# Two buffers for delta, du and B and C by the chunk's parity, in a Mamba, expert and attention kernel

## The chip, the core and the metric

The kernel runs on one core of a Trainium2 chip. The metric is the device time of one execution in microseconds; lower is better. The engines are TensorE (PE, with its weight loads PEld), VectorE (DVE), ScalarE (ACT), GpSimd (POOL) and SyncE (SP, which issues the DMAs).

## The reference

Two sequences of 2048 tokens with 256 features pass through four layers, each with a residual and a layer norm. The change is in the first:

```python
xz = xn @ W_in
x_br, z = jnp.split(xz, 2, axis=-1)
# xc: causal convolution of x_br with 4 taps
xb = jax.nn.silu(jnp.transpose(xc, (0, 2, 1)))
Bm = xb @ W_b
Cm = xb @ W_c
delta = jax.nn.softplus(xb @ W_delta + b_delta)
A_bar = jnp.exp(delta[..., None] * A)
Bx = delta[..., None] * Bm[:, :, None, :] * xb[..., None]
def step(h, inp):
    a_t, bx_t, c_t = inp
    h = a_t * h + bx_t
    y_t = jnp.sum(h * c_t[:, None, :], axis=-1)
    return (h, y_t)
...
out = y * jax.nn.silu(z) @ W_out
```

Behind it come a mixture of four experts (a router, then per expert two products with a Gelu between, all four computed and weighted), the projections q, k and v of a 16-head attention, the attention itself, and a last feed-forward layer.

## The kernel before

The first stage (`mamba_moe_qkv`, the first 1800 us) goes through 8 chunks of 512 tokens. The inner width of 512 stands on the partitions as four blocks of 128. An iteration i works on up to four chunks at once: the scan of chunk i, the front part of chunk f = i+1 (norm, `project_x`, `conv`, `project_bc`, `project_delta`, softplus), output projection, router and experts of chunk m = i-1, and the projections q, k, v of chunk q = i-2. Iterations run from -1 to 9; 3 to 5 are one loop, the others are written out. Each engine's program is one fixed order, written by hand, and waits on semaphores.

An iteration has 16 slots n, one per state of the scan:

- VectorE in slot n, for each of four blocks: `b_times` (L1231), du times B's row, which lies in a PSUM bank, and `scan` (L1238) over 512 steps with the decays. Between block 1 and 2 ("the middle") and behind block 3 and `keep_state` (L1244, "the end") stands other work: `down` (L1316, adds an expert's output to the sum), `gated` (L1250, y times the gate, middle of slot 0), `norm1_stats` (L1256 and more, middle of slot 2), `conv` (L1191), `keys` (L1333, the added keys, middle of slot 7), `weigh` (router weights, end of slot 6), `split_bias` (L1344, end of slot 9), `split_bc` (L1199 to L1206, end of slot 14: B and C as three bf16 parts into `bc3`), `deltas` (L1216, two halves, then du in two halves, L1222; end of slot 15).
- TensorE in slot n: parts of the projections and experts. `up` (L722) fills three PSUM banks in turn, which ScalarE empties by Gelus (L1005); `down` (L746) follows. `broadcast(c, n)` (L598) spreads row n of B over the partitions. It waits until VectorE has used row n-2, since two banks alternate. Slot n ends with the broadcast of row n+2; rows 0 and 1 of the next chunk come at the end of slot 15.
- ScalarE in slot n: first the decays (L913) of slot n+1, which need VectorE's scan of slot n-1 for their buffer, then copies and Gelus. In slots 12 to 14 `copy_delta` (L965, L966) writes the projected delta into `pre` and its absolute value into `soft`, and `soft_exp`, `soft_log` make the softplus' second term.
- GpSimd in slot n: `times_c` (L1437), h times C's row, and `add_y` (L1448), both four instructions, once VectorE has ended slot n. VectorE's scan of slot n waits for `add_y` of slot n-2; `gated` waits for that of slot 15.

`delta`, `du` and `bc3` have one buffer. So `deltas` has to wait for the chunk's last decays and last `b_times`, and `split_bc` for its last broadcast. The decays of the next chunk wait for both halves of `deltas`. The buffer `soft` also serves chunk q: `cr` (the cross products), `kb_f` (a bias per head); `kb_parts` has its own.

`START` gives, for iterations 8 and 9, how many products of the first attention heads are put between; the change leaves it alone.

## Time and profile before

| | us |
|---|---|
| median of 3 runs | 3821.85 (3819.26 to 3822.27) |
| the profiled execution | 3819.2, its span 3817.4 |
| first stage, of the span | about 1830 |
| PE busy over the span | 3385.6 (89%) |
| DVE busy | 2945.8 (77%) |
| ACT busy | 2222.2 (58%) |
| POOL busy | 1508.8 (40%), nearly all of it in the first stage |
| granted TensorE clock, mean | 0.95 |

An engine's busy time over the whole span is a mean over two stages with different limits; the change touches the first alone. Four views of it are used: the instructions of one line in a stretch (when an iteration begins), the busy time in a stretch, the waits of an engine (who ended them, how long), and the timeline, where each row is a run of instructions of one line, with its start, its length and, in brackets, the idle time ahead of it and what ended that.

### The profile page before, as it was taken

To read this page: it belongs to the slowest core of one execution; us is meant where nothing else is said; L and a number is where in the kernel's file an instruction comes from. 1 tells how busy PE (TensorE), PEld (TensorE's weight loads), DVE (VectorE), ACT (ScalarE), POOL (GpSimd) and SP (SyncE) were. 2 spreads that over 40 slices of the span, in tenths; PEclk is the share of its full clock that TensorE was granted. 3 is DMA by queue.
4 is the path that set the end of the run, shared out by engine and by line. 5 is a ranking of instruction groups with operands and counts; after the bars stand their busy time and mean duration, and the time that the engine had idled before them with its cause. 6 is when DMAs were issued, how large, how long until landed. Compare 5 with 4: busy or idle time off the path is not lost. (4 is left out here: it accounts for less than half of the span.)

```text
span 3817.4 us, 50051 instructions
## 1 busy us (share of the span) xinstructions
PE 3385.6 (89%) x14561; PEld 1587.7 (42%) x14561; DVE 2945.8 (77%) x3571; ACT 2222.2 (58%) x3640; POOL 1508.8 (40%) x1294
## 2 busy tenths in 40 slices
PE   4339899898888989899979999999999999999998
PEld 1115555454554546455533232323232323233666
DVE  5898797978879787985438888888788888887343
ACT  5345565656556565553127777777677777776221
POOL 3988787887878788885010000000000000000110
PEclk8669999999999999999989999999999999999999
DMA  2111122122222212223111000000000000001010
GB/s 104 32 38 61 56 71 91 61 87 72 72 65 75 85 61 83 70 80 127 56 46 50 18 18 18 18 18 18 19 18 18 18 18 18 18 18 35 22 33 28
DMA packets 111209, 183.03 MB, mean 48 GB/s; under 512 B 14623, under 2 KB 84663, under 8 KB 102393
## 3 DMA queue, kind: packets, MB, share of 16 engines
q1 hardware_dynamic: 110969, 180.13, 14.9%
q8 instruction: 114, 1.87, 0.2%
q14 instruction: 126, 1.03, 0.1%
HBM read 153.99 MB, written 26.09 MB: 47 GB/s over the span
## 5 line engine op out<-in xcount | busy, mean ns | idle before, releaser
L1894 DVE TENSOR_REDUCE tile_max<-ps 128x1 f32<-128x1024 f32 x1028 | 1210.9, 1220 | 253.3 <-PE ps L1685 250.5
L1835 ACT ACTIVATE probs<-ps 128x512 f32<-128x512 f32 x2056 | 1115.9, 598 | 374.4 <-PE ps L1699 348.7
L1437 POOL TENSOR_TENSOR vals<-vals,c_sb 128x512 f32<-128x512 f32 x512 | 673.0, 1346 | 275.9 <-DVE state L1244 275.8
L1238 DVE TENSOR_TENSOR_SCAN vals<-stacks,state,ps 128x512 f32<-128x512 f32 x512 | 655.0, 1279 | 99.2 <-POOL heads_v L1448 28.1
L1699 PE MATMUL ps<-stacks 101*128 101x512 bf16 x2056 | 708.1, 382 | 13.6 <-ACTq L1842 12.4
L1448 POOL TENSOR_TENSOR heads_v<-heads_v,vals 128x512 f32<-128x512 f32 x512 | 638.9, 1280 | 8.7 <-issue 0.2
L1685 PE MATMUL ps<-stacks 99*128 99x512 bf16 x2056 | 614.4, 379 | 0.0
L1709 PE MATMUL ps<-probs,heads_v 128*32 128x512 f32 x4096 | 547.7, 605 | 5.5 <-issue 5.5
L231 POOL COPY heads_v<-vals 128x256 f32 (+1 forms) x32 | 12.6, 401 | 1345.1 <-PE ps L1709 1322.0
L746 PE MATMUL ps<-e_w,hid 128*128 128x256 f32 x2048 | 472.2, 389 | 38.4 <-issue 33.4
L722 PE MATMUL ps<-x1T,e_w 128*128 128x512 f32 x1024 | 467.5, 601 | 35.4 <-ACT hid L1005 35.4
L1699 PEld LDWEIGHTS ps<-stacks 101*128 101x128 bf16 x2056 | 198.1, 96 | 649.7 <-ACT probs L1835 431.4
L746 PEld LDWEIGHTS ps<-e_w,hid 128*128 128x128 f32 x2048 | 399.8, 196 | 120.0 <-issue 62.2
L913 ACT ACTIVATE stacks<-stacks,neg_a 128x512 f32<-128x512 f32 x512 | 335.0, 714 | 178.5 <-DVE vals L1238 163.1
L1005 ACT ACTIVATE hid<-ps,cols 128x512 f32<-128x512 f32 x288 | 190.6, 687 | 374.5 <-PE ps L722 351.9
L1231 DVE TENSOR_TENSOR ps<-stacks,ps 128x512 f32<-128x512 f32 x512 | 353.6, 691 | 15.4 <-PE ps L598 1.3
L722 PEld LDWEIGHTS ps<-x1T,e_w 128*128 128x128 f32 x1024 | 192.2, 192 | 264.5 <-issue 196.6
L1685 PEld LDWEIGHTS ps<-stacks 99*128 99x128 bf16 x2056 | 201.4, 98 | 179.4 <-issue 1.9
L598 PE MATMUL ps<-bc,sel 96*128 96x512 bf16 x128 | 53.0, 415 | 213.2 <-DVE ps L1231 194.7
L1709 PEld LDWEIGHTS ps<-probs,heads_v 128*32 128x32 f32 x4096 | 80.7, 108 | 200.4 <-ACT probs L1835 178.3
L1316 DVE SCALAR_TENSOR_TENSOR x_tok<-ps,cw,x_tok 128x256 f32<-128x256 f32 x128 | 55.4, 474 | 130.7 <-PE ps L746 130.7
L651 PE MATMUL ps<-vals,w_delta 128*128 128x512 f32 x256 | 117.9, 606 | 7.2 <-ACT soft L966 4.0
(181 smaller groups left out, 2941.0 us busy)
## 6 DMA issues: line engine op xcount, KB each, us to landing
e_w<-in_e_w SPq DMA_DIRECT2D x64, 1024.0 KB, 7.0
c_sb<-scratch_c SPq DMA_DIRECT2D x128, 256.0 KB, 3.4
stacks<-scratch_q SPq DMA_DIRECT2D x210, 64.0 KB
stacks<-scratch_k SPq DMA_DIRECT2D x210, 64.0 KB
scratch_q<-parts SPq DMA_DIRECT2D x16, 384.0 KB, 4.3
scratch_k<-parts SPq DMA_DIRECT2D x16, 384.0 KB, 4.2
xr<-scratch_x SPq DMA_DIRECT2D x10, 512.0 KB, 4.2
xn_tok<-in_x SPq DMA_DIRECT2D x8, 512.0 KB, 4.9
```

Of the source, the lines that this page charges most:

```text
L722: last = mm(bank(key), e_w1[:, e % 2, k, i * P:(i + 1) * P], x1T[:, k, :], start=k == 0, stop=k == KD - 1)
L746: last = mm(ps[:, DOWN_BANK[at], i * D:(i + 1) * D], hid[:, k, (2 * pair + i) * P:(2 * pair + i + 1) * P], e_w2[:, e % 2, k, :], start=k = ...
L913: fn(decay[:, n % 2, m, :], delta[:, m, :], ACT.Exp, scale=neg_a[:, n * DB + m:n * DB + m + 1]).then_inc(s["decay_ready"], 1)
L1231: v.tensor_tensor(ps[:, 0, :], du[:, m, :], ps[:, 2 + n % 2, :], ALU.mult).then_inc(s["bx_ready"], 1)
L1238: v.tensor_tensor_scan(h[:, n % 2, m, :], decay[:, n % 2, m, :], ps[:, 0, :], state[:, n, m:m + 1], ALU.mult, ALU.add).then_inc(s["h_ready ...
L1437: last = nc.gpsimd.tensor_tensor(h[:, n % 2, m, :], h[:, n % 2, m, :], c_sb[:, n % C_RING, :], ALU.mult)
L1448: last = nc.gpsimd.tensor_tensor(y[:, m, :], y[:, m, :], h[:, n % 2, m, :], ALU.add)
L1685: last = mm(ps[:, slot(side) + i, :], qs[0:K_MAX, j, t * P:(t + 1) * P], ks[0:K_MAX, j, k * CH:(k + 1) * CH], start=True, stop=True)
L1699: mm(ps[:, S_BANK[i], :], ks[0:K_ALL, j, step * P:(step + 1) * P], qs[0:K_ALL, j, qc * CH:(qc + 1) * CH], start=True, stop=True).then_inc( ...
L1709: last = mm(ps[qc * VW:(qc + 1) * VW, AV_BANK, :], vh[:, j, step, :], probs[:, step % 2, qc, :], start=step == 0, stop=step == KT - 1)
L1835: fn(probs[:, step % 2, qc, :], ps[:, S_BANK[i], :], ACT.Exp)\
L1894: v.tensor_reduce(tile_max[:, t, half:half + 1], ps[:, slot(side):slot(side) + PAIR, :].rearrange("p a n -> p (a n)"), AX.X, ALU.max).then ...
```

## The change

1. `delta`, `du` and `bc3` get two buffers each, taken by the chunk's parity. One `delta` lies where `pre` was, one `du` is the old `soft`. ScalarE now writes the projected delta straight into the `delta` buffer and the absolute value into the `du` buffer; `deltas` and du work in place. The buffers of chunk q (`cross_of`, `bias_of`, `bias_parts`) lie in the `du` buffer that the scan does not use just then (`spare_of`). The waits follow: `copy_delta` also waits for the stored head bias, and for du and `b_times` of the chunk two before.
2. VectorE's order: `split_bc` at the end of slot 12 (was 14); `deltas` by halves, the first in the middle of slot 14, the second at its end (both were at the end of slot 15), each with its du; the `down` of expert 2's second pair at the end of slot 14 (was its middle); `keys` at the end of slot 6 ahead of `weigh` (was the middle of slot 7), but for iteration 8. Decays of slot 0 wait for their half.
3. TensorE's order: the broadcast of row n+1 stands inside slot n; that of row n+2 stood at its end. Row 1 of a chunk is broadcast in slot 0, between the two `down`.
4. Iterations 3 to 5 are written out.

TensorE, iteration 2, slots 6 to 7, before (L598 broadcast, L722 `up`, L813 `add_keys`, L746 `down`):

```order
L598 MATMUL ps<-bc,sel 128x512
L722 MATMUL ps<-x1T,e_w 128x512 x8
L813 MATMUL ps<-soft,wqs 128x512 x2
L598 MATMUL ps<-bc,sel 128x512
L722 MATMUL ps<-x1T,e_w 128x512 x8
L746 MATMUL ps<-e_w,hid 128x256 x16
L598 MATMUL ps<-bc,sel 128x512
```

and now (L606, L734, L825, L758; `bc_0` is one of the two `bc3`):

```order
L734 MATMUL ps<-x1T,e_w 128x512 x8
L606 MATMUL ps<-bc_0,sel 128x512
L825 MATMUL ps<-soft,wqs 128x512 x2
L734 MATMUL ps<-x1T,e_w 128x512 x8
L606 MATMUL ps<-bc_0,sel 128x512
L758 MATMUL ps<-e_w,hid 128x256 x32
L606 MATMUL ps<-bc_0,sel 128x512
```

Each slot's broadcast has moved ahead of `add_keys` and of `down`, and names the next row instead of the one behind it.

TensorE, iteration 2, from the end of slot 10 to the middle of slot 12, before (L702 `turn_weights`, L641 `project_bc`, L651 `project_delta`):

```order
L722 MATMUL ps<-x1T,e_w 128x512 x8
L598 MATMUL ps<-bc,sel 128x512
L702 MATMUL ps<-ident,cw 4x128 x4
L722 MATMUL ps<-x1T,e_w 128x512 x8
L641 MATMUL ps<-vals,w_bc 96x512 x4
L598 MATMUL ps<-bc,sel 128x512
L651 MATMUL ps<-vals,w_delta 128x512 x4
L746 MATMUL ps<-e_w,hid 128x256 x8
```

and now (from slot 10's second `up`; L714, L653, L663):

```order
L606 MATMUL ps<-bc_0,sel 128x512
L734 MATMUL ps<-x1T,e_w 128x512 x8
L714 MATMUL ps<-ident,cw 4x128 x4
L734 MATMUL ps<-x1T,e_w 128x512 x8
L606 MATMUL ps<-bc_0,sel 128x512
L653 MATMUL ps<-vals,w_bc 96x512 x4
L663 MATMUL ps<-vals,w_delta 128x512 x4
L758 MATMUL ps<-e_w,hid 128x256 x8
L606 MATMUL ps<-bc_0,sel 128x512
```

The row for slot 12 was broadcast ahead of slot 11's work; it now comes behind `turn_weights` and `up` of slot 11.

VectorE, iteration 2, slot 14 from its middle, `split_bc`, and the first block of slot 15, before:

```order
L1316 SCALAR_TENSOR_TENSOR x_tok<-ps,cw,x_tok 128x256 x2
L1231 TENSOR_TENSOR ps<-stacks,ps 128x512
L1238 SCALAR_TENSOR_TENSOR vals<-stacks,state,ps 128x512
L1231 TENSOR_TENSOR ps<-stacks,ps 128x512
L1238 SCALAR_TENSOR_TENSOR vals<-stacks,state,ps 128x512
L1244 TENSOR_SCALAR state<-vals,cols 128x4
L1199 CAST bc<-bc_f 96x512
L1201 TENSOR_TENSOR q_f<-bc_f,bc 96x512
L1203 CAST q_f<-q_f 96x512
L1205 COPY bc<-q_f 32x512
L1206 TENSOR_TENSOR bc<-q_f 32x512
L1231 TENSOR_TENSOR ps<-stacks,ps 128x512
```

and now, from block 1 of slot 14 to its end (L1256 delta, L1258 du, L1266 `b_times`, L1273 scan, L1351 `down`):

```order
L1266 TENSOR_TENSOR ps<-stacks,ps 128x512
L1273 SCALAR_TENSOR_TENSOR vals<-stacks,state,ps 128x512
L1256 SCALAR_TENSOR_TENSOR vals<-vals,soft 128x1024
L1258 TENSOR_TENSOR soft<-vals 128x1024
L1266 TENSOR_TENSOR ps<-stacks,ps 128x512
L1273 SCALAR_TENSOR_TENSOR vals<-stacks,state,ps 128x512
L1266 TENSOR_TENSOR ps<-stacks,ps 128x512
L1273 SCALAR_TENSOR_TENSOR vals<-stacks,state,ps 128x512
L1279 TENSOR_SCALAR state<-vals,cols 128x4
L1351 SCALAR_TENSOR_TENSOR x_tok<-ps,cw,x_tok 128x256 x2
L1256 SCALAR_TENSOR_TENSOR vals<-vals,soft 128x1024
L1258 TENSOR_TENSOR soft<-vals 128x1024
```

`down` moved from the middle to the end; both halves of delta and du now stand in this slot; `split_bc` (L1241 to L1248 now) stands at the end of slot 12.

The diff, cut to what the text speaks of:

```diff
-        pre = sh.vals[:, 3 * CH * DB:].rearrange("p (b t) -> p b t", b=DB)
-        soft = sb("soft", [P, DB, CH])
-        delta = blocks_of[:, 2 * CH * DB:3 * CH * DB].rearrange("p (b t) -> p b t", b=DB)
-        du = blocks_of[:, 3 * CH * DB:].rearrange("p (b t) -> p b t", b=DB)
+        deltas_at = [blocks_of[:, 2 * CH * DB:3 * CH * DB].rearrange("p (b t) -> p b t", b=DB),
+                     sh.vals[:, 3 * CH * DB:].rearrange("p (b t) -> p b t", b=DB)]
+        soft_own = sb("soft", [P, DB, CH])
+        dus_at = [blocks_of[:, 3 * CH * DB:].rearrange("p (b t) -> p b t", b=DB), soft_own]
...
-        bc3 = sb("bc3", [6 * NS, CH], BF16)
+        bc3_at = [sb(f"bc3_{i}", [6 * NS, CH], BF16) for i in range(2)]
...
+        def spare_of(c):
+
+            return dus_at[(c + 1) % 2] if c + 2 < chunks else soft_own
+
+        def cross_of(c):
+            return spare_of(c)[0:CX2, 0, :]
+
+        def bias_of(c):
+            return spare_of(c)[0:NH, 1, :]
+
+        def bias_parts(c):
+            return spare_of(c)[0:NH, 2:4, :].bitcast(BF16).rearrange("p a t -> p (a t)")[:, 0:3 * CH]\
+                .rearrange("p (i t) -> p i t", i=3)
...
         def iterations(engine, iteration):
 
 
-            for i in (-1, 0, 1, 2):
-                iteration(i)
-            with engine.Fori(3, chunks - 2) as i:
-                iteration(i)
-            for i in (chunks - 2, chunks - 1, chunks, chunks + 1):
+            for i in range(-1, chunks + 2):
                 iteration(i)
...
@@ -595,8 +603,12 @@
                 if n == 0:
                     pe.wait_ge(s["bc_steps"], c * 5 + 5)
                 at_least(pe, s["bx_ready"], DB * (c * NS + n - 1))
-                mm(ps[:, 2 + n % 2, :], sel[:, n:n + 1].to_broadcast([6 * NS, P]), bc3[:], start=True, stop=True)\
+                mm(ps[:, 2 + n % 2, :], sel[:, n:n + 1].to_broadcast([6 * NS, P]), bc3_at[c % 2][:], start=True, stop=True)\
                     .then_inc(s["b_mm"], 1)
+
+            def next_b(i, n):
+                if inside(i):
+                    broadcast(i, n + 1)
...
                 for n in range(NS):
-                    quota[0] = START.get((i, n), 0) if isinstance(i, int) else 0
-                    if n == 0 and inside(q):
-                        down(q, NE - 1, 0)
-                        down(q, NE - 1, 1)
-                    if n == 1 and inside(m):
-                        project_out(m)
+                    quota[0] = START.get((i, n), 0)
+                    if n == 0:
+                        if inside(q):
+                            down(q, NE - 1, 0)
+                        if inside(i):
+                            broadcast(i, 1)
+                        if inside(q):
+                            down(q, NE - 1, 1)
+                    if n == 1:
+                        if inside(m):
+                            project_out(m)
+                        next_b(i, n)
                     if n == 2:
                         if inside(q):
                             turn_x2(q)
                             project_v(q)
+                        next_b(i, n)
                         if inside(i):
                             project_z(i)
...
                         if inside(m):
                             router(m)
+                        next_b(i, n)
                         if inside(f):
                             project_x(f, (2, 3))
-                    if n == 11 and inside(m):
-                        turn_weights(m)
-                    if n in (8, 10) and inside(m):
-                        down(m, (n - 8) // 2, 1)
+                    if n in (6, 7):
+                        if inside(m):
+                            up(m, 0, n - 6)
+                        next_b(i, n)
+                        if n == 6 and inside(q):
+                            add_keys(q, i)
+                        if n == 7 and inside(m):
+                            down(m, 0, 0)
+                    if n in (8, 10):
+                        if inside(m):
+                            down(m, (n - 8) // 2, 1)
+                        next_b(i, n)
+                        if inside(m):
+                            up(m, n // 2 - 3, 0)
+                        if n == 8 and inside(q):
+                            key_bias(q, i)
+                    if n == 9:
+                        if inside(m):
+                            up(m, 1, 1)
+                        next_b(i, n)
+                        if inside(m):
+                            down(m, 1, 0)
+                    if n == 11:
+                        if inside(m):
+                            turn_weights(m)
+                            up(m, 2, 1)
+                        next_b(i, n)
+                        if inside(f):
+                            if inside(m):
+                                pe.wait_ge(s["down_read"], m * 2 * NE + 4)
+                            if inside(q):
+                                pe.wait_ge(s["kadd_read"], (q + 1) * KD)
+                            project_bc(f)
                     if n in (12, 13):
                         for part in range(2):
                             if inside(f):
                                 project_delta(f, 2 * (n - 12) + part)
                             if inside(m):
                                 down(m, 2, n - 12, (part,))
-                    if inside(m):
-                        for j in range(2 * NE):
-                            if n == SLOT_OF_UP[j]:
-                                up(m, j // 2, j % 2)
-                    if n in (7, 9) and inside(m):
...
+                            if part == 0:
+                                next_b(i, n)
+                    if n in (14, 15):
                         if inside(m):
-                            pe.wait_ge(s["down_read"], m * 2 * NE + 4)
-                        if inside(q):
-                            pe.wait_ge(s["kadd_read"], (q + 1) * KD)
-                        project_bc(f)
-                    if n == 14 and inside(m):
-                        base(m)
-                    if inside(i) and n + 2 < NS:
-                        broadcast(i, n + 2)
+                            up(m, 3, n - 14)
+                        if n == 14:
+                            next_b(i, n)
+                            if inside(m):
+                                base(m)
                     if n == 15 and inside(f):
                         broadcast(f, 0)
-                        broadcast(f, 1)
...
-                    if n == 0 and m == 0:
-                        act.wait_ge(s["delta_ready"], (c + 1) * 2)
+                    if n == 0:
+                        act.wait_ge(s["delta_ready"], c * 2 + m // 2 + 1)
                     at_least(act, s["h_ready"], (c * NS + n - 2) * DB + m + 1)
-                    fn(decay[:, n % 2, m, :], delta[:, m, :], ACT.Exp,
+                    fn(decay[:, n % 2, m, :], deltas_at[c % 2][:, m, :], ACT.Exp,
...
                     at_least(act, s["kb_steps"], 5 * (c - 2))
-                    at_least(act, s["delta_ready"], c * 2)
+                    at_least(act, s["kb_stored"], 16 * (c - 2))
+                    at_least(act, s["du_ready"], 2 * (c - 1))
+                    at_least(act, s["bx_ready"], (c - 1) * NS * DB)
                 src = ps[:, delta_bank(c, m), :]
-                fn(pre[:, m, :], src, ACT.Identity, bias=col("b_delta", m)).then_inc(s["pre_ready"], 1)
-                fn(soft[:, m, :], src, ACT.Abs, bias=col("b_delta", m)).then_inc(s["abs_ready"], 1)
+                fn(deltas_at[c % 2][:, m, :], src, ACT.Identity, bias=col("b_delta", m)).then_inc(s["pre_ready"], 1)
+                fn(dus_at[c % 2][:, m, :], src, ACT.Abs, bias=col("b_delta", m)).then_inc(s["abs_ready"], 1)
...
             def split_bc(c):
                 dve.wait_ge(s["bc_copied"], c + 1)
                 at_least(dve, s["parts_steps"], 8 * (c - 3) + 4)
-                at_least(dve, s["b_mm"], c * NS)
-                steps = s["bc_steps"]
+                at_least(dve, s["b_mm"], (c - 1) * NS)
+                steps, bc3 = s["bc_steps"], bc3_at[c % 2]
...
-            def deltas(c):
-                at_least(dve, s["decay_ready"], c * NS * DB)
-                for i in range(2):
-                    half = slice(2 * i, 2 * i + 2)
-                    if i == 0:
-                        dve.wait_ge(s["pre_ready"], (c + 1) * DB)
-                    dve.wait_ge(s["soft_ready"], c * 4 + 2 * i + 2)
-                    v.scalar_tensor_tensor(delta[:, half], pre[:, half], 0.0, soft[:, half],
-                                           ALU.max, ALU.add).then_inc(s["delta_ready"], 1)
-                at_least(dve, s["bx_ready"], c * NS * DB)
-                for i in range(2):
-                    half = slice(2 * i, 2 * i + 2)
-                    dve.wait_ge(s["delta_ready"], c * 2 + i + 1)
-                    v.tensor_tensor(du[:, half], delta[:, half], xb[:, half], ALU.mult)\
-                        .then_inc(s["du_ready"], 1)
+            def deltas(c, i):
+                half = slice(2 * i, 2 * i + 2)
+                delta, soft = deltas_at[c % 2][:, half], dus_at[c % 2][:, half]
+                dve.wait_ge(s["pre_ready"], c * DB + 2 * i + 2)
+                dve.wait_ge(s["soft_ready"], c * 4 + 2 * i + 2)
+                v.scalar_tensor_tensor(delta, delta, 0.0, soft, ALU.max, ALU.add).then_inc(s["delta_ready"], 1)
+                dve.wait_ge(s["delta_ready"], c * 2 + i + 1)
+                v.tensor_tensor(soft, delta, xb[:, half], ALU.mult).then_inc(s["du_ready"], 1)
...
-                    if n == 7 and inside(q):
+                    if n == 7 and i == chunks:
                         keys(q)
+                    if n == 14 and inside(f):
+                        deltas(f, 0)
                     if inside(m):
-                        for j in range(6):
+                        for j in range(5):
                             if n == SLOT_OF_DOWN[j] + 1:
                                 down(m, j // 2, j % 2)
...
+                    if n == 6 and inside(q) and i != chunks:
+                        keys(q)
                     if n == 6 and inside(m):
                         weigh(m)
...
                     if n == 9 and inside(q):
                         split_bias(q)
+                    if n == 12 and inside(f):
+                        split_bc(f)
+                    if n == 14 and inside(m):
+                        down(m, 2, 1)
                     if n == 14 and inside(f):
-                        split_bc(f)
-                    if n == 15 and inside(f):
-                        deltas(f)
+                        deltas(f, 1)
                     for _ in range(START.get((i, n), 0) if isinstance(i, int) else 0):
                         start_head(begun[0])
                         begun[0] += 1
```

## Rows read from the trace of the kernel before

**Rows 1.** One line's instructions in a stretch: `deltas` at four iterations' starts (ns min/median/max).

```profile
L1216 DVE SCALAR_TENSOR_TENSOR stacks<-vals,soft x2: 1220/1760/2299, 440.1 to 441.2; 128x1024 f32<-128x1024 f32 x2
...
L1216 DVE SCALAR_TENSOR_TENSOR stacks<-vals,soft x2: 1219/1754/2289, 661.8 to 663.0; 128x1024 f32<-128x1024 f32 x2
...
L1216 DVE SCALAR_TENSOR_TENSOR stacks<-vals,soft x2: 1224/1758/2293, 1328.1 to 1329.2; 128x1024 f32<-128x1024 f32 x2
...
L1216 DVE SCALAR_TENSOR_TENSOR stacks<-vals,soft x2: 1219/1756/2292, 1549.7 to 1550.8; 128x1024 f32<-128x1024 f32 x2
```

**Rows 2.** Busy time by stretch, iteration 4: length, PE, PEld, DVE, ACT, POOL busy.

```profile
892.00:1114.00 222.00, 195.52 (x636) 115.81 (x636) 186.37 (x232) 129.44 (x186) 182.73 (x156) 0.96 0.22 74
```

**Rows 3.** Waits of VectorE from 884 to 1106: us, times, longest.

```profile
DVE x_tok L1316 <- PE ps L746: 18.8, 4, 8.5
DVE vals L1238 <- ACT stacks L913: 4.8, 3, 2.0
DVE ps L1231 <- issue: 1.1, 1, 1.1
...
DVE kb_parts L1344 <- ACT soft L1059: 0.6, 1, 0.6
```

**Rows 4.** Waits of TensorE in the same stretch.

```profile
PE ps L598 <- DVE ps L1231: 11.0, 4, 6.0
PE ps L746 <- issue: 6.5, 2, 6.2
PE ps L722 <- ACT hid L1005: 5.3, 4, 1.7
```

**Rows 5.** Timeline of VectorE, iteration 4: start, length, line, [idle before].

```profile
898.22 2.29 DVE L1250 TENSOR_TENSOR gate<-heads_v,gate 128x2048 f32<-128x2048 f32 x1
...
920.65 1.20 DVE L1256 SCALAR_TENSOR_TENSOR x_tok<-hid,ps 128x1024 f32<-128x1024 f32 x1
...
1029.72 0.88 DVE L1316 SCALAR_TENSOR_TENSOR x_tok<-ps,cw,x_tok 128x256 f32<-128x256 f32 x2 [5.09 <-PE ps L746]
...
1044.00 1.10 DVE L1244 TENSOR_SCALAR state<-vals,cols 128x4 f32<-128x4 f32 x1
...
1058.72 1.28 DVE L1238 TENSOR_TENSOR_SCAN vals<-stacks,state,ps 128x512 f32<-128x512 f32 x1 [2.02 <-ACT stacks L913]
...
1070.65 0.88 DVE L1316 SCALAR_TENSOR_TENSOR x_tok<-ps,cw,x_tok 128x256 f32<-128x256 f32 x2 [8.53 <-PE ps L746]
...
1084.64 0.88 DVE L1316 SCALAR_TENSOR_TENSOR x_tok<-ps,cw,x_tok 128x256 f32<-128x256 f32 x2 [4.62 <-PE ps L746]
...
1106.08 3.44 DVE L1216 SCALAR_TENSOR_TENSOR stacks<-vals,soft 128x1024 f32<-128x1024 f32 x2
...
1109.45 4.51 DVE L1222 TENSOR_TENSOR stacks<-stacks,vals 128x1024 f32<-128x1024 f32 x2
```

**Rows 6.** Timeline of TensorE, iteration 4.

```profile
948.37 0.39 PE L598 MATMUL ps<-bc,sel 96*128 96x512 bf16 x1 [2.12 <-DVE ps L1231]
...
989.53 9.67 PE L746 MATMUL ps<-e_w,hid 128*128 128x256 f32 x32 [6.21 <-issue]
...
999.25 7.07 PE L746 MATMUL ps<-e_w,hid 128*128 128x256 f32 x32
...
1052.15 3.60 PE L641 MATMUL ps<-vals,w_bc 128*96 128x512 f32 x8
```

**Rows 7.** Timeline of GpSimd, slot 7 of iteration 4.

```profile
994.73 4.96 POOL L1437 TENSOR_TENSOR vals<-vals,c_sb 128x512 f32<-128x512 f32 x4 [5.80 <-DVE state L1244]
999.77 4.94 POOL L1448 TENSOR_TENSOR heads_v<-heads_v,vals 128x512 f32<-128x512 f32 x4
```

**Rows 8.** Waits of VectorE in iterations 0, 1 and 7, one row each.

```profile
DVE vals L1238 <- POOL heads_v L1448: 7.6, 10, 1.9
...
DVE x_tok L1316 <- PE ps L746: 18.0, 3, 8.6
...
DVE x_tok L1316 <- PE ps L746: 4.9, 2, 4.6
```

36 lines of the change are left out of this document (15 added, 21 removed).

## The prediction

> **What bounds the kernel now.** I read the starts of one instruction per chunk first, since they give the length of an iteration, then the waits of VectorE and TensorE in one iteration, then the timelines, and last the waits of the iterations that differ. `deltas` (L1216) starts once an iteration: at 440.1, 661.8, 1328.1 and 1549.7 [rows 1]. So iteration 2 took 221.7 us, the passes 3 to 5 of the loop (1328.1-661.8)/3 = 222.1 each, and iteration 6 221.6. The reader is to see that nothing in such an iteration is full: in 222 us TensorE is busy 195.5, VectorE 186.4 and GpSimd 182.7 [rows 2]. The three take turns.
>
> In iteration 4 (from 884) VectorE waits 18.8 us for TensorE's `down` products, 4.8 for ScalarE's decays [rows 3]. The long ones lie in the second half: 5.09 in slot 10, 8.53 in slot 13, 4.62 in slot 14 [rows 5]. There TensorE is late. In the first half it is the other way: TensorE waits 11.0 us at B's broadcasts for VectorE, and 6.5 with no releaser named [rows 4]. The largest of these, 6.21 us at 989.53, stands before the first `down` of slot 7 [rows 6]; that instruction needs `kadd_read`, which VectorE gives in `keys` in the middle of slot 7, so I put it down to `keys`. The 32 matmuls behind this wait took 9.67 us, the next 32 took 7.07 [rows 6]: 2.6 us more, which I read as the granted clock having dropped in the pause. So both engines lose at different ends of a chunk to an order that lets neither run ahead.
>
> **The change, part by part.** I walked the engines' new orders through iterations 4 and 5 with the durations of the trace, slot by slot. What sets the pace in it is a cycle with two legs: TensorE from `norm1_stats` (slot 2, end of L1256 at 920.65+1.20 = 921.85 [rows 5]), for which `project_z` waits, to the end of the last `up` of slot 11, and VectorE from slot 12 on to the next L1256.
>
> TensorE's leg is now 1052.15-921.85 = 130.3 us [rows 5, 6].
> - `keys` goes from the middle of slot 7 to the end of slot 6. The 6.21 goes, and the 2.6 of slow matmuls: -8.8. VectorE's added wait is for `add_keys`; it ends some 3 us before VectorE is there by my walk, so it costs nothing; behind it stand `weigh` and slot 7.
> - The broadcast that slot 5's `router` had to follow now comes behind it: 2.12 [rows 6] goes.
> - TensorE now gets close to ScalarE, whose Gelus stand behind decays that need VectorE's last slot. I put 1.5 us of new waits there, from two or three of the size of the 1.3 mean in [rows 4] (5.3 in 4). They may be 0 to 5.
> - B(12) was at the end of slot 10, and is now behind the second `up` of slot 11: 0.4 us of its own, and VectorE's slot 12 can't begin before it.
> Sum: 130.3-8.8-2.1+1.5+0.4 = 121.3.
>
> VectorE's leg. From the end of slot 11 (1044.00+1.10 = 1045.1) to the first `deltas` (1106.08) are 61.0 us, with waits of 2.02, 8.53 and 4.62 in them [rows 5] and one of 0.8 (the 4.8 for ScalarE are three waits; the longest is 2.0, and one such lies in slot 4 [rows 3, 5]): 45.0 of work, `split_bc` included. The change puts `split_bc` ahead of slot 13, `deltas(0)` into the middle of slot 14 in place of the `down` read there, and that read and `deltas(1)` at its end. TensorE, some 10 us further ahead than before, has both products by then; so all of these waits go. Of the moved work ScalarE's two logarithms are needed: the walk has them ready 4 and 3 us before VectorE asks. If TensorE were not ahead, the 8.53 would still be filled with `split_bc`'s 6.5.
> - The four instructions of `deltas` and `du` are the same in number. They took 3.44+4.51 = 7.95 [rows 5]. One alone takes 1.226, one beside GpSimd's products 2.297 [rows 1]. Now all four have GpSimd beside them: 4 x 2.30 = 9.2. Between nothing (7.95) and that I take 9.2.
> - Then slot 15 ends and slot 0 opens at once, with no 7.95 between them. But `gated` needs GpSimd's two passes over slot 15, 4.96+4.94 = 10.0 with the gap [rows 7]. VectorE has only 4.2 (two blocks) and 0.85 (`down`) before it: it will wait 5.1 us here, where it waited nothing to 1.2. This is the wait that takes the place of the boundary. The price is 0 if VectorE loses the time before, 5.1 as the walk has it.
> - From `gated` (898.22) to the end of L1256 (921.85) is 23.6 us [rows 5], unchanged.
> Sum: 45.0+9.2+10.1+23.6 = 87.9.
>
> The cycle is 121.3+87.9 = 209.2 us, against 222.1: 12.9 less. On it VectorE waits some 4 us for B(12) and 5.1 for GpSimd in place of 23.3 us. Five iterations (2 to 6) have all parts: 64 us.
>
> Iteration 1 has no attention part; TensorE isn't late at B(12). It loses 18.0 of waits for `down` [rows 8], gains 5.1 and 1.2: -11.7. Iteration 7 makes no next chunk: of its 4.9 [rows 8] 4.6 goes, as `keys` is earlier there too, and GpSimd, which bounds its second half, would start that much earlier. Iteration 0 has only GpSimd to wait for, 7.6 in all [rows 8]; the moved work fills the one or two such waits at its end, and the first decays may start at the first half: -2. Iterations 8 and 9 and all of the attention stage keep their order: 0.
>
> **Written-out iterations.** Iterations 2 and 6 already are written out in the kernel before, and take 221.7 and 221.6 against 222.1 for a looped pass [rows 1]: 0.45 us x 3 = 1.4 us of gain at most, inside the rounding. The one mark of the loop is the 1.1 us before L1231 with no releaser [rows 3]. The Trainium skill (Runtime: NRT & Kernel Launch, Instruction fetch mechanics) says that straight code is fetched ahead and that a taken branch may stall the fetch; by that the loop's 1.1 us would go three times, 3.4 us, against the 1.4 of the trace.
>
> The Trainium skill (SBUF — State Buffer, Who interferes with whom) has a rule that speaks against the change: a VectorE instruction with two SBUF inputs and a GpSimd one that reads SBUF exclude each other, and the later one stands for the whole of the other. By that rule no placing of `deltas` beside GpSimd is free, and the sum would have the 9.2 that I took anyway from the row.
>
> **Sum.** 64+11.7+4.6+2 = 82 us. The profiled execution took 3819.2 (span 3817.4), so 3737; the median of the runs shown is 3821.85, 2.7 above it, and 82 less is **3740**.
>
> **Rivals.**
> 1. TensorE's leg is not binding. Then VectorE's own chain counts: 222.1-18.8-2.8-1.1-0.6+5.1+1.2 = 205.1, 17 us per iteration, 85+18 = 103 in all: **3719**. For it: TensorE's 195.5 busy holds slow stretches that would go. Against: the walk finds B(12) late, by the 4.1 us between this and 209.2.
> 2. B comes late. In the kernel before TensorE ends slot 11's `up` at 1052.15 while VectorE opened slot 12 at 1045.0 [rows 5, 6]: 7.1 us late for the new place. If the 6.21 at `keys` only turns into waits for ScalarE's Gelus (three banks), TensorE's leg is 127.5, the cycle 215.4, the gain 6.7: 5 x 6.7+17 = 50, **3772**.
> 3. Slower. The same 7.1 us at three slots (21.3) plus 5.1 for GpSimd is 26.4, more than the 23.3 (18.8+2.8+1.1+0.6) that goes; each late slot of VectorE then holds TensorE at its next broadcast, and so the lead never builds. +3.1 x 6 = 19: **3841**. It decides from the point where new waits of VectorE pass 23.3 us per iteration. Against: TensorE does lose the 6.21, and in the first half it has the broadcasts early.
> 4. The change does not do what it says: the shared buffer (`spare_of`, whose users must be stored before `copy_delta`) holds ScalarE back and the deltas come no sooner: **3822**. Against: that buffer's last user, the store of the heads' bias, is issued behind slot 9, and `copy_delta` comes in slot 12.
>
> **Chances and range.** Forecast 0.50 (3726 to 3754); rival 1 0.18; rival 2 0.22; rival 3 0.05; rival 4 0.05. The range reaches from beyond rival 1 to beyond rival 2, 3705 to 3785, and leaves out about 0.15. A measurement of this kernel can tell 0.2% (8 us) from no change: faster 0.90, same 0.05, slower 0.05.
>
> **What would show it.** Right: `deltas` starts come 209 us apart; the wait of 6 us before the first `down` is gone; VectorE's waits for `down` fall from 18.8 to under 3; a wait of about 5 us for GpSimd before `gated`, and one of about 4 for the broadcast before slot 12's first product. Rival 1: no wait for the broadcast. Rival 2: several such waits, and TensorE waiting for ScalarE by 5 us or more. Wrong altogether: VectorE waiting for ScalarE's logarithm at `deltas`, or TensorE's clock staying low after the new pause behind `project_out`. The least sure terms are the 1.5 us of Gelu waits and whether the lead of TensorE holds through slots 8 to 11.

## The result, and the profile after

| | before | after |
|---|---|---|
| median | 3822.06 us (3819.26 to 3822.87) | 3752.88 us (3751.89 to 3753.47) |
| ratio | | 0.982, 95% interval 0.9803 to 0.9837 |
| span of the profiled execution | 3817.4 | 3751.7 |

The forecast was 3740 in a range of 3705 to 3785. The kernel is faster by 69 us; 82 were forecast.

I measure an iteration from the end of `norm1_stats`' first instruction (L1256 before, L1291 after; middle of slot 2) to the same point of the next one.

| stretch | before | after | gain | forecast |
|---|---|---|---|---|
| to the first `norm1_stats` | 265.1 | 265.6 | -0.5 | 2 (iteration 0) |
| iteration 1 to 2 | 212.7 | 212.1 | 0.6 | 11.7 |
| the next five | 221.9, 222.3, 222.0, 221.8, 221.6 | 212.0, 209.7, 211.2, 211.0, 209.8 | 55.8 | 64 |
| iteration 7 to 8 | 184.2 | 179.1 | 5.1 | 4.6 |
| from there to the end of the span | 2045.9 | 2041.2 | 4.7 | 0 |
| sum | 3817.4 | 3751.7 | 65.7 | 82 |

VectorE's waits in iteration 4 of the changed kernel, from 866 to 1077 (us in total, times, longest):

```profile
DVE ps L1266 <- PE ps L606: 6.1, 2, 5.8
DVE gate L1285 <- POOL heads_v L1489: 4.6, 1, 4.6
DVE vals L1273 <- ACT stacks L952: 1.9, 1, 1.9
DVE vals L1273 <- POOL heads_v L1489: 0.6, 1, 0.6
DVE x_tok L1351 <- PE ps L758: 0.5, 1, 0.5
```

The 18.8 us for `down` [rows 3] are 0.5. In their place stand two waits: one for B's broadcast and one for GpSimd. TensorE's waits in the same stretch:

```profile
PE ps L734 <- ACT hid L1046: 6.1, 4, 1.9
PE ps L777 <- ACT x_tok L113: 4.1, 1, 4.1
PE ps L678 <- DVE x_tok L1351: 1.5, 1, 1.5
PE ps L758 <- DVE x_tok L1351: 1.0, 1, 1.0
```

The 11.0 us at broadcasts and the 6.5 with no releaser [rows 4] are gone. The busy time is what it was [rows 2], in 211 us, not 222 (length, PE, PEld, DVE, ACT, POOL busy):

```profile
866.00:1077.00 211.00, 194.16 (x635) 114.90 (x635) 187.26 (x233) 129.19 (x186) 183.58 (x156) 0.97 0.24 78
```

The places on VectorE's timeline that answer to [rows 5]:

```profile
875.84 2.29 DVE L1285 TENSOR_TENSOR gate<-heads_v,gate 128x2048 f32<-128x2048 f32 x1 [4.63 <-POOL heads_v L1489]
...
898.22 1.20 DVE L1291 SCALAR_TENSOR_TENSOR x_tok<-hid,ps 128x1024 f32<-128x1024 f32 x1
...
1022.36 0.70 DVE L1266 TENSOR_TENSOR ps<-stacks,ps 128x512 f32<-128x512 f32 x1 [5.83 <-PE ps L606]
...
1053.49 2.17 DVE L1256 SCALAR_TENSOR_TENSOR vals<-vals,soft 128x1024 f32<-128x1024 f32 x1
1055.70 2.19 DVE L1258 TENSOR_TENSOR soft<-vals 128x1024 f32<-128x1024 f32 x1
...
1062.94 1.83 DVE L1256 SCALAR_TENSOR_TENSOR vals<-vals,soft 128x1024 f32<-128x1024 f32 x1
1064.81 2.17 DVE L1258 TENSOR_TENSOR soft<-vals 128x1024 f32<-128x1024 f32 x1
...
1109.45 1.20 DVE L1291 SCALAR_TENSOR_TENSOR x_tok<-hid,ps 128x1024 f32<-128x1024 f32 x1
```

And on TensorE's, for [rows 6]: all 64 matmuls of slot 7 in 13.98 us with nothing before them, and B(12) right behind the last `up` of slot 11.

```profile
961.70 13.98 PE L758 MATMUL ps<-e_w,hid 128*128 128x256 f32 x64
...
1020.12 1.98 PE L734 MATMUL ps<-x1T,e_w 128*128 128x512 f32 x4 [1.06 <-ACT hid L1046]
1021.94 0.38 PE L606 MATMUL ps<-bc,sel 96*128 96x512 bf16 x1
```

From 899.42 (898.22+1.20) to 1022.36, when VectorE has B(12), are 122.9 us: TensorE's leg, forecast 121.3. From there to 1110.65 are 88.3: VectorE's leg, forecast 87.9.

At its start TensorE's leg is no longer released by `norm1_stats`. `project_z` starts at 899.72, 0.30 us behind the end of L1291, and no wait for L1291 stands before it. What holds TensorE is the 4.08 us before `turn_x2` (L777), the transposes that come ahead of `project_v` and `project_z`:

```profile
882.74 4.96 POOL L1478 TENSOR_TENSOR vals<-vals,c_sb 128x512 f32<-128x512 f32 x4 [6.93 <-DVE state L1279]
...
889.06 0.20 POOL L1563 TENSOR_TENSOR ln_t<-ln_half,ln_r 128x4 f32<-128x4 f32 x1
...
889.29 2.08 ACT L113 ACTIVATE x_tok<-x_tok,ln_t,ln_r 128x256 f32<-128x256 f32 x4 [3.79 <-POOL ln_t L1563]
...
891.42 1.97 PE L777 MATMUL ps<-ident,x_tok 128*128 128x128 f32 x8 [4.08 <-ACT x_tok L113]
...
894.12 5.54 PE L768 MATMUL ps<-x1T,wqkv 128*128 128x512 f32 x8 [0.73 <-issue]
```

VectorE ends slot 0 late, because `gated` waited; then GpSimd's `times_c` starts, and behind it stand the small instructions (L1558 to L1563) of chunk q's norm, which ScalarE's norm needs. So the wait for GpSimd reaches TensorE by two ways, over `norm1_stats` and over `turn_x2`, that end within 0.3 us of each other.

### The profile page after: what moved, and what is told of

It is laid out like the page before. It is cut to its first block and busy times, and to the rows that moved or that the text cites. A ratio compares the mean times of both kernels' runs of the same rounds, so it can differ in the third digit from the quotient of the medians.

```text
span 3751.7 us, 48756 instructions
## 1 busy us (share of the span) xinstructions
PE 3370.5 (90%) x14561; PEld 1576.1 (42%) x14561; DVE 2948.3 (79%) x3571; ACT 2221.7 (59%) x3640; POOL 1513.4 (40%) x1294
## 5 line engine op out<-in xcount | busy, mean ns | idle before, releaser
L1478 POOL TENSOR_TENSOR vals<-vals,c_sb 128x512 f32<-128x512 f32 x512 | 659.8, 1320 | 187.0 <-DVE state L1279 187.0
L1273 DVE TENSOR_TENSOR_SCAN vals<-stacks,state,ps 128x512 f32<-128x512 f32 x512 | 655.1, 1279 | 80.2 <-POOL heads_v L1489 21.0
L1489 POOL TENSOR_TENSOR heads_v<-heads_v,vals 128x512 f32<-128x512 f32 x512 | 654.7, 1310 | 8.7 <-issue 0.2
L734 PE MATMUL ps<-x1T,e_w 128*128 128x512 f32 x1024 | 468.4, 602 | 43.1 <-ACT hid L1046 41.6
L758 PE MATMUL ps<-e_w,hid 128*128 128x256 f32 x2048 | 457.2, 381 | 14.6 <-DVE x_tok L1351 12.5
L758 PEld LDWEIGHTS ps<-e_w,hid 128*128 128x128 f32 x2048 | 390.6, 191 | 90.7 <-issue 36.7
L734 PEld LDWEIGHTS ps<-x1T,e_w 128*128 128x128 f32 x1024 | 191.5, 191 | 281.1 <-issue 204.1
L952 ACT ACTIVATE stacks<-stacks,neg_a 128x512 f32<-128x512 f32 x256 | 167.7, 713 | 99.7 <-DVE vals L1273 99.3
L952 ACT ACTIVATE stacks<-vals,neg_a 128x512 f32<-128x512 f32 x256 | 167.2, 713 | 92.8 <-DVE vals L1273 87.3
L1266 DVE TENSOR_TENSOR ps<-soft,ps 128x512 f32<-128x512 f32 x256 | 176.8, 691 | 35.3 <-PE ps L606 29.1
L1266 DVE TENSOR_TENSOR ps<-stacks,ps 128x512 f32<-128x512 f32 x256 | 176.9, 691 | 26.7 <-PE ps L606 20.6
L606 PE MATMUL ps<-bc,sel 96*128 96x512 bf16 x128 | 52.7, 413 | 124.9 <-DVE ps L1266 110.4
```

What stands on the lines that cost most here:

```text
L734: last = mm(bank(key), e_w1[:, e % 2, k, i * P:(i + 1) * P], x1T[:, k, :], start=k == 0, stop=k == KD - 1)
L758: last = mm(ps[:, DOWN_BANK[at], i * D:(i + 1) * D], hid[:, k, (2 * pair + i) * P:(2 * pair + i + 1) * P], e_w2[:, e % 2, k, :], start=k = ...
L952: fn(decay[:, n % 2, m, :], deltas_at[c % 2][:, m, :], ACT.Exp, scale=neg_a[:, n * DB + m:n * DB + m + 1]).then_inc(s["decay_ready"], 1)
L1266: v.tensor_tensor(ps[:, 0, :], dus_at[c % 2][:, m, :], ps[:, 2 + n % 2, :], ALU.mult).then_inc(s["bx_ready"], 1)
L1273: v.tensor_tensor_scan(h[:, n % 2, m, :], decay[:, n % 2, m, :], ps[:, 0, :], state[:, n, m:m + 1], ALU.mult, ALU.add).then_inc(s["h_ready ...
L1478: last = nc.gpsimd.tensor_tensor(h[:, n % 2, m, :], h[:, n % 2, m, :], c_sb[:, n % C_RING, :], ALU.mult)
```

## The experiments

The theory is that of the prediction, the cycle of two legs. Its rivals are that the gain lies in the moved deltas, in the later broadcasts, or in the written-out program. Kernels that differ in one edit from the changed one are compared with its 3752.9, the others with the kernel before, which took 3820.9 to 3822.9 beside them.

| kernel | median (lowest to highest) | steady iteration | against |
|---|---|---|---|
| before + early keys | 3789.2 (3782.6 to 3793.6) | 217.9 | before: -32 |
| before, written out | 3817.5 (3814.8 to 3821.3) | 221.9 | before: -3.4 |
| changed, keys back | 3803.6 (3796.5 to 3808.0) | 219.2 | changed: +51 |
| changed, split back | 3783.4 (3781.8 to 3786.7) | 215.8 | changed: +30 |
| changed, deltas back | 3772.8 (3771.3 to 3774.2) | 214.6 | changed: +20 |
| changed, broadcasts back | 3740.2 (3733.4 to 3746.9) | 208.6 | changed: -13 |
| changed, B(12) earlier | 3741.1 (3737.5 to 3745.6) | 208.2 | changed: -12 |
| changed, `gated` later | 3731.0 (3726.7 to 3743.5) | 206.1 | changed: -22 |
| broadcasts and keys back | 3775.6 (3772.2 to 3776.4) | 215.0 | broadcasts back: +35 |
| broadcasts and deltas back | 3742.4 (3741.3 to 3748.1) | 210.6 | broadcasts back: +2 |
| B(12) earlier, `gated` later | 3727.4 (3725.2 to 3732.5) | 207.7 | `gated` later: -4 |
| broadcasts back, `gated` later | 3723.8 (3717.8 to 3727.6) | 205.9 | changed: -29 |

A steady iteration is the mean of the three from the third `norm1_stats` to the sixth: 222.0 in the kernel before, 210.7 in the changed one.

**Keys alone, in the kernel before.**

```diff
-                    if n == 7 and inside(q):
+                    if n == 7 and isinstance(i, int) and i == chunks:
                         keys(q)
...
+                    if n == 6 and inside(q) and not (isinstance(i, int) and i == chunks):
+                        keys(q)
                     if n == 6 and inside(m):
                         weigh(m)
```

> The kernel before with one edit: `keys` at the end of slot 6, not in the middle of slot 7. Theory of two legs: before, the cycle runs over TensorE from `norm1_stats` to the `down` product of slot 14 and back over VectorE; the pause of 6.2 us before slot 7's first `down` and the slow matmuls behind it lie on it, so an iteration gets 6 to 8.8 us shorter, some 39 us in all: 3783 (3774 to 3792), and VectorE's waits for `down` fall from 18.8 to about 12. Rival, that the early keys bring nothing without the later broadcasts (TensorE waits 11 us for VectorE there, and would wait longer): 3812 to 3822.

Measured 3789.2, 32 us less. This small edit alone makes nearly half of the gain. But a steady iteration got only 4.1 us shorter, where the theory had 6 to 8.8: in three of the five (2 to 6) the router's second product in slot 5 takes 5.5 to 5.7 us, in the other two 3.7. VectorE's waits in iteration 4, 873 to 1091: those for `down` fell from 18.8 to 13.2.

```profile
DVE x_tok L1316 <- PE ps L746: 13.2, 3, 8.4
DVE vals L1238 <- POOL heads_v L1450: 2.8, 2, 2.0
```

The one of 5.09 in slot 10 has gone but for 0.2, while those of slots 13 and 14 stay. Iteration 1, which has no keys, hardly changes (211.6 against 212.7).

**Keys back, in the changed kernel** (the same lines undone).

> The changed kernel with `keys` back in the middle of slot 7. Theory of two legs: TensorE's leg grows from 122.9 to 129 to 131 us, VectorE's wait for B(12) from 5.8 to 12 to 14, an iteration by 6 to 8: 5 x 7 + 4 = 39 us, 3792 (3783 to 3798). Rival, that the earlier deltas and split made most of the gain, and the keys little: 3755 to 3765.

Measured 3803.6, 51 more: the rival of 3755 to 3765 is out, and the cost is above the range that I gave. TensorE shows what comes back, 5.29 us and 16.57 us for the 64 matmuls that take 13.98 without the pause:

```profile
981.06 16.57 PE L758 MATMUL ps<-e_w,hid 128*128 128x256 f32 x64 [5.29 <-issue]
```

That is 7.9 us; the steady iteration grew by 8.5, iteration 7 by 9.7. VectorE meets the delay in five waits of 1.2 to 5.4 us in slots 9 to 12, and not in one of 12 to 14 at slot 12 as I had it. Four of the five are for broadcasts, since each now stands behind a `down` or `up` that is late.

**Broadcast of row 12 earlier.**

```diff
                             turn_weights(m)
-                            up(m, 2, 1)
                         next_b(i, n)
+                        if inside(m):
+                            up(m, 2, 1)
```

> The changed kernel with the broadcast of row 12 ahead of the second `up` of slot 11, not behind it. Theory of two legs: the 5.8 us that VectorE waits at slot 12 go; the next thing that TensorE is asked for is slot 13's first `down` product, which is 3.8 us ahead of its read now and so would be waited for by 2 us. So 3.8 to 5.8 us per iteration in 5 iterations and up to 6.4 in iteration 1: 22 to 35 us, 3724 (3718 to 3731). Rival, that TensorE is the bound by its own work and Gelus and the wait only moves to slot 13: 3745 to 3753.

Measured 3741.1, 12 less: between both. The wait of 5.8 went, and 4.1 us of it came back at once. VectorE in slots 13 and 14 of iteration 4:

```profile
1028.70 0.88 DVE L1352 SCALAR_TENSOR_TENSOR x_tok<-ps,cw,x_tok 128x256 f32<-128x256 f32 x2 [2.22 <-PE ps L758]
...
1035.81 0.70 DVE L1267 TENSOR_TENSOR ps<-stacks,ps 128x512 f32<-128x512 f32 x1 [1.87 <-PE ps L606]
```

The 2.22 was forecast (2). I hadn't seen the 1.87: B(14) stands behind slot 13's first `down`, so it is late as well. Iteration 1 got 5.7 us shorter (206.4 against 212.1), the steady ones 2.5.

**All broadcasts back.**

```diff
-                        if inside(i):
-                            broadcast(i, 1)
...
-                        next_b(i, n)
...
+                    if inside(i) and n + 2 < NS:
+                        broadcast(i, n + 2)
                     if n == 15 and inside(f):
                         broadcast(f, 0)
+                        broadcast(f, 1)
```

> The changed kernel with all broadcasts where they were (row n+2 at the end of slot n, rows 0 and 1 of the next chunk at the end of slot 15). Theory of two legs: B(12) is early, as with the one broadcast moved, and the 2.1 us that slot 5's `router` lost come back, but TensorE's leg isn't binding then: 3725 (3715 to 3740). Rival, that the later broadcasts were what let TensorE run ahead, so that undoing them gives back a part of the gain: 3760 to 3775.

Measured 3740.2, its slowest run below the changed kernel's fastest. So the later broadcasts, one of the four parts of the change, cost some 13 us in this kernel; 7.2 us of the difference between the two traces lie in iteration 1. With them TensorE waits no more for VectorE at a broadcast, but the longest of these pauses only changes its name: with the old places TensorE waits 4.06 us for VectorE at the broadcast just ahead of `turn_x2`, with the new ones 4.08 for ScalarE at `turn_x2` itself. And VectorE waits for the later broadcasts at slot 12, and that is on the cycle.

**Deltas back at the end of slot 15.**

```diff
-                    if n == 14 and inside(f):
-                        deltas(f, 0)
...
-                    if n == 14 and inside(f):
+                    if n == 15 and inside(f):
+                        deltas(f, 0)
                         deltas(f, 1)
```

> The changed kernel, with its two buffers, but both halves of `deltas` and du at the end of slot 15 as before. Theory that the earlier deltas only exchange one wait for another, now that TensorE is ahead by the keys and the split: the 4.63 us that `gated` waits for GpSimd go under the 8 us of deltas, the deltas get 0.4 shorter with GpSimd idle at their end, and the slot 14 product (at 1055.9 us in iteration 4's trace) is still there before its read: 5.0 us less per iteration in 7 iterations, 3718 (3715 to 3735). Rival, that taking the deltas out of the chunk's boundary is what made the gain: the waits of slots 13 and 14 for TensorE come back, 4.6 to 8 us more per iteration, 3775 to 3790.

Measured 3772.8, 20 more, and neither was right. The wait for GpSimd fell from 4.63 to 1.23 as I said. But VectorE, 8 us sooner at slot 15, ran into a broadcast that neither theory had (timeline of VectorE, slots 14 and 15 of iteration 4):

```profile
1060.14 0.69 DVE L1266 TENSOR_TENSOR ps<-stacks,ps 128x512 f32<-128x512 f32 x1 [1.42 <-PE ps L606]
...
1076.32 0.69 DVE L1266 TENSOR_TENSOR ps<-stacks,ps 128x512 f32<-128x512 f32 x1 [6.65 <-PE ps L606]
```

B(15) now stands behind the first `up` of slot 14. In the changed kernel the deltas fill just this time.

**Broadcasts and deltas back** (both diffs).

> The changed kernel with the broadcasts at their old places and both halves of `deltas` at the end of slot 15. With the new places the deltas at the end cost 20 us, and VectorE waited 6.0 to 6.7 us at slot 15 for B(15). Theory A, that TensorE as a whole is behind there: with B(15) early, VectorE waits about 6 us for the product of `base` in slot 15 instead (in the kernel with the old broadcasts it is ready 1.9 us ahead of its read, and the read would come 8.4 earlier); with the 2.4 and 1.1 for GpSimd and TensorE in slot 0 gone, 2.6 us more per iteration, 3758 (3750 to 3765). Theory B, that it was the place of B(15) alone: no such wait, 3720 (3715 to 3730).

Measured 3742.4, with the broadcasts alone 3740.2, whose runs spread over 13 us: no difference that could be told by medians; the steady iteration is 1.9 us longer. Of the two theories the mechanism of A is there and its size isn't:

```profile
1056.98 1.49 DVE L1327 TENSOR_TENSOR x_tok<-ps,x_tok 128x512 f32<-128x512 f32 x2 [5.08 <-PE ps L724]
```

VectorE waits 5.08 us for `base` in slot 15, where it had waited 6.65 for B(15). So the place of B(15) makes the smaller part of that wait: TensorE as a whole is behind there. With the old broadcasts the moved deltas exchange this wait for a longer one at `gated` (2.38 us, with the deltas back 1.21) and smaller ones in slot 0.

**Split back at the end of slot 14.**

```diff
-                    if n == 12 and inside(f):
+                    if n == 14 and inside(f):
                         split_bc(f)
```

> The changed kernel with `split_bc` back at the end of slot 14. Theory of two legs: slot 13's product and B(14) then are 2.4 and 3.1 us late, so slot 14 opens when it does now (within 0.4 us), and the 6.25 us of the split come behind it: 5.9 us more per iteration in 6 iterations, 3788 (3778 to 3792). Rival, that the split is VectorE's work wherever it stands: 3748 to 3758.

Measured 3783.4, 30 more, in the range. The two waits are where they were put, 2.32 and 1.87 us (VectorE, slots 13 and 14 of iteration 4); the first line shows that the wait at slot 12 is nearly what it was:

```profile
1035.78 0.70 DVE L1266 TENSOR_TENSOR ps<-stacks,ps 128x512 f32<-128x512 f32 x1 [5.00 <-PE ps L606]
...
1054.16 0.88 DVE L1351 SCALAR_TENSOR_TENSOR x_tok<-ps,cw,x_tok 128x256 f32<-128x256 f32 x2 [2.32 <-PE ps L758]
...
1061.27 0.70 DVE L1266 TENSOR_TENSOR ps<-stacks,ps 128x512 f32<-128x512 f32 x1 [1.87 <-PE ps L606]
```

**`gated` at the end of slot 0.**

```diff
-                    if n == 0 and inside(m):
-                        gated(m)
...
+                    if n == 0 and inside(m):
+                        gated(m)
                     if n == 0 and inside(q):
                         down(q, NE - 1, 1)
                         norm2_stats(q)
```

> The changed kernel with `gated` at the end of slot 0, not in its middle. Theory of two legs: the wait of 4.63 us for GpSimd is filled with the two blocks (4.2) behind it, `gated` starts at the same time, and `norm1_stats` comes 4.2 us sooner, since `project_out` is done 11 us before it: 4.2 x 7 = 29 us, 3724 (3720 to 3732). Rival, that TensorE's own chain bounds the iteration and VectorE only meets its next wait 4 us sooner: 3748 to 3753.

Measured 3731.0, 22 less (the profiled execution 3726.7, 27 less). `gated` stands with no wait before it:

```profile
865.32 2.29 DVE L1285 TENSOR_TENSOR gate<-heads_v,gate 128x2048 f32<-128x2048 f32 x1
```

The steady iteration fell by 4.6 us, to 206.1. VectorE's leg makes that: 83.3 us in the mean of the five, where it was 87.8, with TensorE's leg as long as before (122.8 and 122.9). So the new wait for GpSimd was on the cycle for nearly its whole length, and two blocks of scan hide it.

**`gated` later, together with each of the other places for broadcasts** (the diffs above joined).

> The changed kernel with both edits: the broadcast of row 12 ahead of slot 11's second `up`, and `gated` at the end of slot 0. `gated` alone gave 22 us, the broadcast alone 12. If TensorE is near its own bound once `gated` is late (in the trace of that kernel it waits 12 us of 205, for ScalarE most of it), the second edit finds little left: VectorE's 4.1 us at slot 12 turn into waits at slot 13 and 14, 1 to 2 us per iteration and 5 in iteration 1: 3721 (3715 to 3728). Rival, that the two add up: 3719 less 5, 3709 (3705 to 3714).

Measured 3727.4, inside the range; the 4 us are within the spread of the runs with `gated` later alone. The second edit finds little left, as the theory has it.

> The changed kernel with the broadcasts at their old places and `gated` at the end of slot 0. The old broadcasts leave a wait of 2.37 us at `gated`, where the new ones leave 4.63, so less is there to fill, and TensorE waits 4.1 us at a broadcast that needs VectorE: 1 to 2.4 us less per iteration than with the old broadcasts alone, 3728 (3723 to 3734). Rival, that both gains add up (12.7 and 21.9): 3718.

Measured 3723.8, between both, and by the median the fastest kernel of all: 0.9739 of the kernel before (0.9723 to 0.9756), and 29 us below the changed one.

**Keys back, with the old broadcasts.**

> The changed kernel with the broadcasts at their old places and `keys` in the middle of slot 7: what is left of the change is the split, the deltas and the buffers. `keys` back alone gave 3803.6, the broadcasts back alone 3740.2. Theory of two legs: TensorE's leg is 7 to 8.8 us longer and binds, the place of B(12) is worth as much as in the other pair or less, since slot 13's product is late too: 3795 (3788 to 3804). Rival, that with the old broadcasts TensorE can take the loss in its lead: 3770 to 3780.

Measured 3775.6, below the one and inside the other. So the keys are worth 35 us with the old broadcasts, 51 with the new, and 32 in the kernel before. Against the kernel before (3822.9 beside it) this one is 47 us faster with neither early keys nor later broadcasts: split, deltas and buffers bring more than the keys, and with the old broadcasts the two parts about add up (32 and 47 make 79; with both it is 81). Since the deltas hardly count there, the 47 point to the split; the split alone was not run. With the new broadcasts the parts don't add: where broadcasts stand behind TensorE's products, a late product holds VectorE up to four times.

**Only written out.**

```diff
-                for i in (-1, 0, 1, 2):
-                iteration(i)
-            with engine.Fori(3, chunks - 2) as i:
-                iteration(i)
-            for i in (chunks - 2, chunks - 1, chunks, chunks + 1):
+            for i in range(-1, chunks + 2):
                 iteration(i)
```

> The kernel before with all iterations written out and nothing else. By the trace of before: 0.45 us for each of the three passes of the loop, 1.4 in all, 3820; the 1.1 us ahead of the first `b_times` of a pass goes. If the pause in the middle of the attention stage (56.4 us between two copies in the kernels with the loop, 52.0 to 53.2 in those without) comes from the layout of the code, 3.5 us more, 3817 (3815 to 3819). Rival, that the written-out program was a large part of the gain: 3790 to 3810.

Measured 3817.5, 3.4 less (a ratio of 0.9981 to 1.0, so hardly to be told from nothing; the two profiled executions differ by 1.5). The iterations are as long as before (221.9): the loop's 1.1 us before L1231 in iteration 4 is gone, but VectorE then waits 1.2 for GpSimd before `gated`. The one thing that is clearly shorter is a pause in the attention stage, between its two sequences. GpSimd's copies around it, in the kernel before:

```profile
2752.68 0.40 POOL L231 COPY heads_v<-vals 128x256 f32 x1 [46.57 <-PE ps L1709]
2808.59 0.40 POOL L231 COPY heads_v<-vals 128x256 f32 x1 [55.51 <-PE ps L1709]
```

in the kernel before, written out:

```profile
2753.37 0.40 POOL L231 COPY heads_v<-vals 128x256 f32 x1 [46.57 <-PE ps L1705]
2806.61 0.40 POOL L231 COPY heads_v<-vals 128x256 f32 x1 [52.83 <-PE ps L1705]
```

and in the changed kernel:

```profile
2690.11 0.40 POOL L231 COPY heads_v<-vals 128x256 f32 x1 [46.58 <-PE ps L1750]
2742.47 0.40 POOL L231 COPY heads_v<-vals 128x256 f32 x1 [51.96 <-PE ps L1750]
```

The step is 55.9 and 56.4 us in the two kernels with a loop, and 52.0 to 53.2 in the twelve without. Why this is so was not tried.

## Why the prediction was right, and where not

**The cycle of two legs: right, but for where TensorE's leg begins.** It is 211.2 us in iteration 4 against 209.2, with the forecast waits in the forecast places: 4.63 for GpSimd (5.1; the rows that it was worked out from give 10.0-4.2-0.85 = 4.9) and 5.83 at slot 12 (4). I had TensorE released by `norm1_stats`; it waits for ScalarE at `turn_x2` and then comes 0.3 us behind `norm1_stats`. That the leg can still be counted from there is luck: the two ways end almost together. The 6.21 before the first `down` is gone with its slow matmuls; that it was `keys` was an inference, and undoing `keys` alone shows it. Rival 1 (no wait at slot 12) and rival 2 (several, 215.4) are out for the steady iterations; so are 3 and 4.

That the total came within 13 us has some luck in it too: the terms for the iterations are 21 us too high together, and 4.7 came from the stretch behind them, which I had at 0.

**The five steady iterations: 55.8 for 64.** The term that was too small is TensorE's leg. Two stretches of low clock stand in it or just ahead of it. Behind the 4.08 us that it waits at `turn_x2` the granted clock is 0.50 (1.2 GHz) from 891.4 to 896, and `project_v` takes 5.54 us, where in the kernel before it took 3.67; with the transposes (1.97, not 1.04) that makes 2.8 us. By this estimate TensorE would else have been at `project_z` first and waited for `norm1_stats`, so it costs the cycle only the 0.3. And in slot 5 the router's second product (32 matmuls) takes 3.9 to 5.0 us in all five, where it took 3.7 in four of five before. The 3.91 stands in an iteration of 209.7 us, the 4.96 in one of 211.2:

```profile
723.88 3.91 PE L704 MATMUL ps<-r_w,hid 128*128 128x4 f32 x32 [0.87 <-ACT hid L1046]
...
933.24 4.96 PE L704 MATMUL ps<-r_w,hid 128*128 128x4 f32 x32 [0.87 <-ACT hid L1046]
```

So the granted clock, which the early `keys` gave back in slot 7, is in part lost again in slot 5. From 900 to 933 us it is 1.00 (2.4 GHz), with waits of 0.87 us before 925.3 and before 933.2; from 933 to 944 it is 0.69 in the mean, between its two levels, and from 944 on 1.00 again. What brings it down there was not tried. In iteration 4 the leg has, against 1.5 us of Gelu waits in the sum, 0.6 for Gelus, 1.2 for this product, 0.9 before the router's first and 0.3 in `project_z`: 3.0.

**Iteration 1: 0.6 for 11.7, the step that failed.** I wrote: "Iteration 1 has no attention part; TensorE isn't late at B(12)". What failed is the second half of it, by which I took all of the 18.0 us for gone and put nothing for broadcasts. Iteration 1 has no `keys` either, so the edit that makes TensorE's leg shorter gives nothing there, while the later broadcasts are there in full. VectorE's waits:

```profile
359.81 0.69 DVE L1266 TENSOR_TENSOR ps<-soft,ps 128x512 f32<-128x512 f32 x1 [3.38 <-PE ps L606]
366.72 0.88 DVE L1351 SCALAR_TENSOR_TENSOR x_tok<-ps,cw,x_tok 128x256 f32<-128x256 f32 x2 [2.69 <-PE ps L758]
373.84 0.69 DVE L1266 TENSOR_TENSOR ps<-soft,ps 128x512 f32<-128x512 f32 x1 [1.89 <-PE ps L606]
...
389.56 0.70 DVE L1266 TENSOR_TENSOR ps<-soft,ps 128x512 f32<-128x512 f32 x1 [6.37 <-PE ps L606]
```

These 14.3 us, 0.7 for the last `down` and 3.3 more for GpSimd before `gated` (4.48, was 1.23) take the place of the 18.0 for `down` [rows 8] and of 1.6 for ScalarE. It is the picture of rival 2, B late at several slots, in the one iteration without `keys`; its condition (Gelu waits in place of the pause at `keys`) is not what made it. The trace of before had it: there, too, the last `up` of slot 11 ended (386.6) 7.3 us after VectorE had opened slot 12 (379.3). With the broadcasts back iteration 1 is 204.9 us, 7.2 shorter.

**Iteration 7: 5.1 for 4.6.** Right in the sum only. The 4.6 for `down` is gone, but VectorE waits 5.51 us for B(12), which I hadn't seen, and the waits at the iteration's end are others (5.01 for `down` and 4.27 for GpSimd in the next slot 0, where they were 1.97 and 7.33).

**Iteration 0: -0.5 for 2.** The first 265 us differ by up to 2.4 us between kernels that have the same order there (267.3 with the keys back, 264.9 with B(12) earlier), so the 2 can't be told.

**Written out: 3.4 for 1.4, and attention 3.5 for 0.** The 0.45 us per pass wasn't there. Nor were three times 1.1: that the medians differ by just the 3.4 that this would give is chance, since the passes are as long as before. The 3.5 that the changed kernel gains in the attention stage, whose order is the same, is the pause above, and 2.7 of it come with writing out alone. The other 1.2 us lie in the last chunk's router and experts (the router's second product took 4.5 us, and takes 3.7).

**The deltas.** Their four instructions took 8.4 us (2.17, 2.19, 1.83, 2.17), not 9.2. I read the 1.2 of [rows 1] as one that stands alone, and that was wrong: it started at 1106.08, 0.12 us before GpSimd, and there GpSimd pays. Its four instructions of 4.96 us take 8.88:

```profile
1106.20 8.88 POOL L1437 TENSOR_TENSOR vals<-vals,c_sb 128x512 f32<-128x512 f32 x4 [5.10 <-DVE state L1244]
```

With this the rule of the Trainium skill (SBUF — State Buffer, Who interferes with whom), that the two exclude each other and the later one stands, agrees on both sides: the instruction that comes second is the long one. The 0.8 us too many hardly matter: put back under the old broadcasts, the deltas change nothing that the medians tell. What I missed is what they stand in for: time in which VectorE would wait for TensorE in slots 14 and 15.

## What to carry to other kernels

Where several engines take turns in a ring, write the cycle down leg by leg, and do so for each kind of iteration: an edit that pays for another's cost (here the early keys for the later broadcasts) must be present in every one. A consumer's read that frees a producer's bank (the keys) is worth moving ahead of other work: here that edit alone gave 32 of 69 us. Ask of each part of a bundle whether the rest is better without it; here the later broadcasts cost 13 us, and the wait that moved deltas make before `gated` is hidden by placing that one instruction two blocks later (22 us).
